# Order of the first loads and of the ahead-of-time keys in a two-layer Perceiver kernel

## Chip, cores and metric

One Trainium2 chip, one core of it (core 0). The metric is the device time of one execution in microseconds (us), the median of several runs. All data are float32 except a few 16-bit integer tiles in the quantized feed-forward layer.

## What is computed

The input is `x`, 64 sequences of 32 rows with 256 features, and a context `ctx` of 64 sequences with 257 rows of 256 features. Six residual steps follow one another, each on a layer-normalized `x`:

```
x = x + L0_xattn(norm(x), ctx)   # causal 32 x 257: only the first 32 context rows count; 16 heads of 16
x = x + L0_attn(norm(x))         # causal attention by offsets, position bias, sigmoid gate
x = x + L0_ffn(norm(x))          # gate/up/down with fake quantization: act_qdq needs max|.| over the whole tensor
x = x + L1_xattn(norm(x), ctx)   # full cross-attention over all 257 context rows
x = x + L1_attn(norm(x))         # causal attention with a Pluecker-line bias
x = x + L1_ffn(norm(x))          # ternary-weight network 256 -> 1024 -> 1024 -> 1024 -> 256
```

In `L0_ffn` each `act_qdq` divides by the largest absolute value of a whole tensor. So the layer has five points (`QX, QG, QU, QS, QO`) at which every column must have been reduced on VectorE and combined over the partitions on GpSimd before anything is scaled; their scales are announced on the semaphore `f0_scale`, 1 to 5.

## The kernel before, in words

The 2048 rows of `x` are 16 tiles (`T`) of 128 rows, kept in SBUF for the whole kernel. The program is written engine by engine: SyncE (the DMA queue), TensorE, ScalarE, VectorE and GpSimd each have one instruction stream in a fixed, hand-written order, and semaphores order them among each other. An instruction waits at the head of its own engine's stream, so whatever stands behind it waits too.

**Attention stages.** `run_lanes` runs the first cross-attention (X0), the first self-attention (A0) and, later, the second self-attention (A1). Four tiles go through a stage together as four lanes, shifted against each other by a quarter of the round, and there are four rounds. Round 0 is unrolled; rounds 1 to 3 are a hardware loop, in which the round number `i` is a register. A tile of X0 begins on VectorE with the statistics (`d_norm`, L1312 and L1315), goes over GpSimd (`rsqrt`, L1804 to L1810) to ScalarE (`a_scale`, L1004), and then to TensorE, which turns it (`p_turn`, L545) and projects it with the X0 weights (`p_project`, L533). The X0 keys and values come from the first 32 context rows of each sequence (`ctxk`).

**First loads (L398 to L423).** SyncE issues all the loads of the start in one row: two tiles of `x`; seven constants, counted on `in_const`; the four X0 weights; `ctxk` of the four lanes; the other 14 tiles of `x`, counted on the same semaphore `in_x`; six later constants; and then all the weights up to A1 and `c_last`. VectorE waits for all seven constants (L1451), makes four small tiles from them (L1452 to L1455), and waits for `in_x` at 32, that is for both loads of `x`, before the first statistics (L1456). TensorE, ScalarE and GpSimd wait for all seven constants as well.

**Keys ahead (L424 to L457, L834 to L852, L1150 to L1181).** Of each group of four sequences, the second cross-attention needs the keys of the fourth one made ahead: there are 16 such projections `j`, in the time of the `L0_ffn` stage. SyncE loads the context `j` (256 KB, `load_ahead`, L432) into one of three buffers; TensorE projects it (L847, eight matmuls) into PSUM bank `(j+1) % 8`; ScalarE evacuates it (`stage_ahead`, L1155, two instructions) into one of four buffers; SyncE stores it to DRAM (`store_ahead`, L437). The queue's order is

```
for j in range(T):
    if j + 3 < T: wait k_ready >= j+1; load_ahead(j+3)
    if j == 10:   wait f0_gj >= 2; load c_ctx[0..3]
    if j >= 1:    store_ahead(j-1)      # waits for k_copied >= j
```

From `j = 8` on, projection `j` also waits for the evacuation of `j-8+1` (its bank), and `stage_ahead(j)` for the store of `j-4` (its buffer). `c_ctx[0..3]` are the contexts of the first four sequences of the second cross-attention. They lie where `gates[0]` and `gates[1]` lay, so their loads wait for the conversions that read these (`f0_gj` at 2).

**Conversions.** ScalarE turns `ups[f]` and `gates[f]`, f = 0 to 5, into 16-bit integers (`f0_up_int` L1141, `f0_gate_int2` L1146, 128x2048 each); VectorE multiplies each pair and reduces its maximum (L1561, then L1492). Two pairs of conversions are held back until `f0_scale` is 3 and 4. `stage_ahead` stands between them in ScalarE's stream: 0 to 3 ahead of the conversions; 4 and 5, then 6, 7 and 8, one group ahead of each of f = 2 to 5; 9 to 15 behind.

**What follows.** GpSimd subtracts the last row from `c_ctx` 0 to 2 (`c_shift`, L1886), and only then comes to `all_max(QO)` (L1852), the reduction over partitions behind the fifth scale. Its instruction is one of another kind than GpSimd's ordinary tensor operations; between the two kinds the trace shows a `MODIFY_POOL_CONFIG` entry. ScalarE, after key 15, evacuates the values of the last rows (L1188) and the keys and values of sequence 0 (L1195, L1201), then waits for `f0_scale` 5 and begins `f0_out_round(0)` (L1182, six instructions). Behind each of these VectorE finishes the quantization (L1488), and TensorE begins the down projection (`f0_down`, L709). Before that TensorE has, in this order: projection 15, the last rows' values, `c_keys(0)` (L731), `c_values(0)` (L737), `c_keys(1)`, `c_values(1)`.

Of the kernel before, what the change touches and what calls it, by code (L numbers as in the profile page):

```python
# [12 lines left out]
ACT = mybir.ActivationFunctionType  # L13
AX = mybir.AxisListType

P = 128
# [4 lines left out]
S = 257  # L21
# [6 lines left out]
NL = 4  # L28
# [15 lines left out]
def perceiver(nc, A, out):  # L44
    ctx = ExitStack()
    with ctx:
        def sb(name, shape, dt=F32):
            return ctx.enter_context(nc.sbuf_tensor(name, shape, dt))

        def sem(name):  # L50
            return ctx.enter_context(nc.semaphore(name))
# [208 lines left out]

        magic = sb("magic", [P, 1])

        ps = ctx.enter_context(nc.psum_tensor("ps", [P, 8, 512], F32))


        in_const, in_later_const = sem("in_const"), sem("in_later_const")
        in_x = sem("in_x")
        in_w = {k: sem(f"in_w_{k}") for k in ("x0", "a0", "nat", "x1", "a1", "ffn")}
# [43 lines left out]

        c_last_in, c_vl_ps, c_vl_done, c_kl_done = map(sem, ("c_last_in", "c_vl_ps", "c_vl_done", "c_kl_done"))
        ctx_in = [sem(f"ctx_in{i}") for i in range(4)]
        ahead_stored = [sem(f"ahead_stored{i}") for i in range(4)]
        k_loaded = sem("k_loaded")
        (k_ready, k_copied, ctx_shifted, v_ready, v_copied, c_s, c_max, c_exp, c_rinv, c_nrm, c_pt, c_ptc,
# [69 lines left out]
        BIAS_V = {X0: colb[:, BV0, :], A0: colb[:, BVA, :], A1: a1_bv[:, :]}  # L387
        N_CONST, N_LATER_CONST = 7, 6
        xl = x[:, :, :].rearrange("p (i l) d -> p i l d", l=NL)
# [7 lines left out]
        def _(sp):  # L397
            sp.dma_start(x[:, 0:2, :], A["x"][:, 0:2, :]).then_inc(in_x, 16)  # L398
            for d, n in ((ident, "ident"), (par, "par"), (mask_hr, "mask_hr"), (mask4, "mask4"),
                         (causal, "causal"), (colb, "colb"), (rowb, "rowb")):  # L400
                sp.dma_start(d[:], A[n]).then_inc(in_const, 16)
# [6 lines left out]

            for l in range(NL):
                load_ctxk(l, 0)  # L410
            sp.dma_start(x[:, 2:T, :], A["x"][:, 2:T, :]).then_inc(in_x, 16)
            for d, n in ((posmask, "posbias"), (a1_bv, "a1_bv"), (a1_bqk, "a1_bqk"), (plscale, "plscale"),
                         (plsign, "plsign"), (w3s, "w3s")):
                sp.dma_start(d[:], A[n]).then_inc(in_later_const, 16)
            for d, n in ((a0_wqkv, "a0_wqkv"), (a0_wg, "a0_wg"), (a0_wout, "a0_wout")):
# [23 lines left out]
            def load_keys(i):  # L439

                after(sp, c_s, 2 * SPT * i)
                sp.dma_start(c_kT[3][:, :, 0:S - 1], k_ahead[i]).then_inc(k_loaded, 16)

# [3 lines left out]
            for j in range(T):  # L447
                if j + 3 < T:
                    sp.wait_ge(k_ready, j + 1)
                    load_ahead(j + 3)  # L450
                if j == 10:
                    sp.wait_ge(f0_gj, 2)
                    for n in range(4):
                        sp.dma_start(c_ctx[n], A["ctxT"][n]).then_inc(ctx_in[n], 16)
                if j >= 1:
                    store_ahead(j - 1)
# [67 lines left out]
        def _(pe):  # L524
# [252 lines left out]
            def c_step(i, u, first, last):  # L777
                n = SPT * i + u
                after(pe, c_exp, G * n)
                if u == 3:  # L780
                    pe.wait_ge(k_loaded, 16 * (i + 1))
                else:
                    pe.wait_ge(k_copied, key_no(3 * i + u))
# [87 lines left out]
            pe.wait_ge(n_q2, 1)  # L871
            pe.wait_ge(c_kl_done, 1)
            pe.wait_ge(c_vl_done, 2)
# [118 lines left out]
        def _(act):  # L992
            af = nc.scalar.activation

            def a_scale(kind, l, n):
# [168 lines left out]
            act.wait_ge(c_vl_done, 1)  # L1164
            stage_ahead(0, 1, 2, 3)
            act.wait_ge(f0_scale, 3)
# [4 lines left out]
            f0_gate_int2(1)  # L1171
            for f, js in zip(range(2, NF0), ((4, 5), (6,), (7,), (8,))):
                stage_ahead(*js)
                f0_up_int(f)
                f0_gate_int2(f)
            stage_ahead(*range(9, T))

# [68 lines left out]
            act.wait_ge(c_x, T)  # L1246
            act.wait_ge(consts_made, 2)
            run_lanes(act, SLOTS1, [
# [53 lines left out]
        def _(dve):  # L1302
# [4 lines left out]
            def d_norm(kind, l, i, n):  # L1307

                if kind == A0:
                    dve.wait_ge(s["x_updated"], tile(i, l))  # L1310
                    stand(dve, "dve")
                v.bn_stats(stats[l][:, :], xl[:, i, l, :]).then_inc(s["stats_ready"], 1)  # L1312
                dve.wait_ge(s["stats_ready"], tile(n, l))
                stand(dve, "dve")
                v.bn_aggr(mv[l][:, :], stats[l][:, :]).then_inc(s["mv_ready"], 1)  # L1315
# [37 lines left out]

            def d_mask(kind, l, i, n):
                dve.wait_ge(s["scores_ready"], tile(n, l))
                mk = posmask if kind == A0 else causal
                if kind != A1:

                    grid = dict(c=4, w=2, k=2 * L)
                    raw = ps[:, 2 * l:2 * l + 2, 0:D].rearrange("p w (c k) -> p w c k", k=2 * L)  # L1360
                    v.tensor_tensor(sc[l].rearrange("p h k -> p (h k)").rearrange("p (c w k) -> p w c k", **grid), raw,
                                    mk[:, :].rearrange("p (c w k) -> p w c k", **grid), ALU.add)\
                        .then_inc(s["scores_masked"], 1)
                    return
                v.scalar_tensor_tensor(sc[l].rearrange("p c k -> p (c k)"), bank[l][0], 0.25, mk[:, :],
                                       ALU.mult, ALU.add).then_inc(s["scores_masked"], 1)
# [87 lines left out]
            for n, at in enumerate((BQ0, BQA)):  # L1454
                v.tensor_scalar(qb[:, n, :], colb[:, at, :], 0.25, None, ALU.mult).then_inc(gate_bias_ready, 1)  # L1455
            dve.wait_ge(in_x, 32)  # L1456

            def enter_a0():
                dve.wait_ge(in_later_const, 16 * N_LATER_CONST)
                v.tensor_tensor(posmask[:, :], posmask[:, :], causal[:, :], ALU.add).then_inc(later_made, 1)  # L1460
# [205 lines left out]
            for u in (0, 1, 3):  # L1666
                r = v.tensor_copy(c_kT[u][:, :, S - 1], colb[:, BK1, :])
            r.then_inc(c_kl_done, 1)
            dve.wait_ge(f0_x, 1 + 1)
# [26 lines left out]
            r.then_inc(consts_made, 1)  # L1696
            dve.wait_ge(consts_made, 2)
            run_lanes(dve, SLOTS1, [
# [98 lines left out]
        def _(pool):  # L1797
# [14 lines left out]
            def bias(l, i, n, k):  # L1812

                pool.wait_ge(s["xn_ready"], tile(n, l))
                p.tensor_tensor(xl[:, i, l, :], xl[:, i, l, :], rowb[:, k, :], ALU.add)\
                    .then_inc(s["x_biased"], 1)
# [113 lines left out]
            last_rsqrt(T - 1)  # L1930
            pool.wait_ge(consts_made, 2)
            pool.wait_ge(later_made, 3)
# [130 lines left out]
```

## Time and profile before

| | us |
|---|---|
| runs: median (lowest to highest of 3) | 1612.7 (1610.29 to 1613.74) |
| the profiled execution, its own time | 1612.98 |
| its span, first to last instruction | 1611.2 |
| TensorE busy | 1465.7 (91%) |
| VectorE busy | 898.6 (56%) |
| ScalarE busy | 712.6 (44%) |
| GpSimd busy | 501.1 (31%) |
| mean granted TensorE clock | 0.978 of full |

How to read it: "busy" is the time in which the engine had an instruction in execution; the share is an average over stages that have different limits. Times within the trace count from the start of the span. In rows of the timeline the first number is the start, the second the length, `x24` means 24 like instructions drawn together, and the bracket tells how long the engine had been idle before and what ended that. The queue's rows (SPq) are the issue of a transfer and not its landing. The kernel's time is a little longer than the span (1.8 us here).

### The profile page before, as it was taken

To read this page: it belongs to the slowest core of one execution; us is meant where nothing else is said; L and a number is where in the kernel's file an instruction comes from. 1 tells how busy PE (TensorE), PEld (TensorE's weight loads), DVE (VectorE), ACT (ScalarE), POOL (GpSimd) and SP (SyncE) were. 2 spreads that over 40 slices of the span, in tenths; PEclk is the share of its full clock that TensorE was granted. 3 is DMA by queue.
4 is the path that set the end of the run, shared out by engine and by line. 5 is a ranking of instruction groups with operands and counts; after the bars stand their busy time and mean duration, and the time that the engine had idled before them with its cause. 6 is when DMAs were issued, how large, how long until landed. Compare 5 with 4: busy or idle time off the path is not lost.

```text
span 1611.2 us, 32991 instructions
## 1 busy us (share of the span) xinstructions
PE 1465.7 (91%) x12564; PEld 1131.0 (70%) x12564; DVE 898.6 (56%) x1897; ACT 712.6 (44%) x1763; POOL 501.1 (31%) x693
## 2 busy tenths in 40 slices
PE   3998996997799999999996788699999999999999
PEld 3887775445677777777773566458867885886887
DVE  2898997479536666666664688634234323422432
ACT  3887775388635554555552455322212212121221
POOL 1444552000125965975652777300000000000000
PEclk9999999998999999999997999899999999999999
DMA  7000000003304153146110000104412330441230
GB/s 285 24 11 2 1 0 21 0 0 118 118 29 143 52 186 127 52 156 221 59 40 1 1 1 0 46 0 142 167 71 92 138 137 13 156 165 59 92 137 13
DMA packets 60509, 123.98 MB, mean 77 GB/s; under 512 B 5008, under 2 KB 15760, under 8 KB 57872
## 3 DMA queue, kind: packets, MB, share of 16 engines
q1 hardware_dynamic: 60432, 122.94, 21.9%
q8 instruction: 50, 0.82, 0.2%
q14 instruction: 27, 0.22, 0.0%
HBM read 108.24 MB, written 14.68 MB: 76 GB/s over the span
## 4 chain that ended last, share of the span: by engine, by line
PE 71%; DVE 11%; POOL 8%; issue 4%; ACT 3%; DMA 1%; SPq 0%; DVEq 0%; POOLq 0%; ACTq 0%
PE ps L921 23%; PE ps L533 17%; PE ps L539 5%; PE ps L737 5%; PE ps L731 4%; PE ps L972 3%; PE ps L757 3%; POOL R L1912 2%; DVE R L1323 2%; DVE R L1618 2%; PE ps L709 2%; POOL R L1894 2%; PE ps L768 2%; PE ps L847 1%; PE ps L602 1%
## 5 line engine op out<-in xcount | busy, mean ns | idle before, releaser
L921 PE MATMUL ps<-R 128*128 128x256 f32 x1792 | 388.6, 379 | 3.4 <-DVE R L1751 3.4
L921 PEld LDWEIGHTS ps<-R 128*128 128x128 f32 x1792 | 340.0, 190 | 52.2 <-issue 6.5
L533 PE MATMUL ps<-R 128*128 128x128 f32 (+1 forms) x1344 | 308.2, 389 | 6.4 <-DVE R L1488 4.8
L533 PEld LDWEIGHTS ps<-R 128*128 128x128 f32 x1344 | 191.3, 195 | 119.3 <-issue 109.6
L1209 ACT ACTIVATE R<-ps,c_nmx 128x257 f32<-128x257 f32 x256 | 118.2, 474 | 126.6 <-DVE c_nmx L1642 126.6
L1894 POOL TENSOR_TENSOR R<-R,c_inv 128x1024 f32<-128x1024 f32 x64 | 121.1, 1892 | 133.2 <-DVE c_inv L1653 133.2
L1618 DVE COPY R<-ps 128x512 f32<-128x512 f32 x128 | 88.1, 688 | 82.1 <-PE ps L757 80.8
L737 PE MATMUL ps<-x_wv,R 128*128 128x256 f32 x512 | 121.1, 379 | 0.0
L1972 POOL TENSOR_SCALAR g_ve<-g_mv 128x4 f32<-128x4 f32 x4 | 0.9, 237 | 345.5 <-DVE g_mv L1713 345.5
L737 PEld LDWEIGHTS ps<-x_wv,R 128*128 128x128 f32 x512 | 92.5, 190 | 10.1
L731 PE MATMUL ps<-R,x_wk 128*128 128x256 f32 x384 | 95.7, 391 | 0.0
L1278 ACT ACTIVATE R<-R,ffn_s 128x256 f32<-128x256 f32 x32 | 16.2, 508 | 167.5 <-DVE R L1758 167.5
L757 PE MATMUL ps<-ident,R 128*128 128x128 f32 x512 | 80.1, 280 | 9.6 <-POOL R L1894 3.8
L1642 DVE TENSOR_REDUCE c_nmx<-ps 128x2 f32<-128x514 f32 x128 | 82.5, 686 | 1.7 <-PE ps L747 1.5
L1265 ACT ACTIVATE R<-ps,ffn_s 128x512 f32<-128x512 f32 x32 | 22.0, 687 | 126.0 <-PE ps L533 126.0
L757 PEld LDWEIGHTS ps<-ident,R 128*128 128x128 f32 x512 | 60.9, 143 | 23.6 <-issue 7.7
L731 PEld LDWEIGHTS ps<-R,x_wk 128*128 128x128 f32 x384 | 68.9, 189 | 12.2 <-issue 0.4
L1492 DVE TENSOR_REDUCE amax<-R 128x1 f32<-128x512 f32 (+1 forms) x60 | 58.4, 1002 | 32.8 <-ACT R L1104 32.3
L1886 POOL TENSOR_TENSOR R<-R 128x512 f32<-128x512 f32 x64 | 68.7, 1074 | 25.2 <-DMA R<-in_ctxT 25.2
L1201 ACT ACTIVATE R<-ps 128x512 f32<-128x512 f32 x64 | 38.4, 600 | 75.3 <-PE ps L737 75.3
L1736 DVE SCALAR_TENSOR_TENSOR R<-ps,ffn_s,R 128x512 f32<-128x512 f32 x32 | 24.0, 750 | 73.0 <-ACT R L1265 73.0
L768 PEld LDWEIGHTS ps<-R 128*32 128x32 f32 x2048 | 32.4, 110 | 44.6 <-DVE R L1618 32.5
(211 smaller groups left out, 2526.2 us busy)
## 6 DMA issues: line engine op xcount, KB each, us to landing
R<-quadrant_sums SPq DMA_DIRECT2D x32, 1024.0 KB, 6.8
R<-in_f_hq SPq DMA_DIRECT2D x32, 768.0 KB, 4.6
R<-in_ctxT SPq DMA_DIRECT2D x64, 257.0 KB, 2.7
R<-in_f_hq SPq DMA_DIRECT2D x8, 1024.0 KB, 8.8
quadrant_sums<-R SPq DMA_DIRECT2D x8, 1024.0 KB, 8.3
R<-in_ctxT SPq DMA_DIRECT2D x16, 256.0 KB, 3.4
k_ahead<-R SPq DMA_DIRECT2D x16, 256.0 KB, 3.4
R<-k_ahead SPq DMA_DIRECT2D x16, 256.0 KB, 3.1
```

The costliest lines, as they stand in the source:

```text
L533: r = mm(dst, w[:, ki, fo * P:(fo + 1) * P], src[:, ki, :], start=(ki == 0), stop=(ki == KI - 1))
L539: r = mm(dst, src[:, ki, :], w[:, ki], start=(ki == 0), stop=(ki == KI - 1))
L731: r = mm(ps[:, 4, fo * D:(fo + 1) * D], x1_wk[:, ki, fo * P:(fo + 1) * P], c_ctx[u][:, ki, 0:2 * P], start=(ki == 0), stop=(ki == KI - 1))
L737: r = mm(ps[:, 5, c * D:(c + 1) * D], c_ctx[u][:, ki, c * P:(c + 1) * P], x1_wv[:, ki, :], start=(ki == 0), stop=(ki == KI - 1))
L757: r = tr(ps[:, 6, at:at + P], c_p[par][:, g, c * P:(c + 1) * P], ident[:])
L768: r = mm(ob[g * L:(g + 1) * L, ki * 2 * L:(ki + 1) * 2 * L], c_v[u][:, c, cols], c_pT[:, g, c, ki * 2 * L:(ki + 1) * 2 * L], start=(c == 0 ...
L921: r = mm(ps[:, 4 * (g % 2) + bk, half * HALF:(half + 1) * HALF], f_wr[g % 3][:, w, ki * P:(ki + 1) * P], src[:, k, ki, :], start=(ki == 0) ...
L1209: af(c_p[par][:, g, :], ps[:, g, 0:S], ACT.Exp, bias=c_nmx[par][:, g:g + 1], accum_out=c_sum[par][:, g:g + 1]).then_inc(c_exp, 1)
L1618: v.tensor_copy(c_pT[:, 2 * k:2 * k + 2, :, :].rearrange("p g c t -> p (g c t)"), ps[:, 6, :])\
L1642: v.tensor_reduce(c_nmx[u % 2][:, 2 * half:2 * half + 2], ps[:, 2 * half:2 * half + 2, 0:S], AX.X, ALU.max, negate=True).then_inc(c_max, 1)
L1886: p.tensor_tensor(c_ctx[u][:, :, 0:S - 1], c_ctx[u][:, :, 0:S - 1], c_ctx[u][:, :, S - 1:S].broadcast_to([P, KI, S - 1]), ALU.subtract).th ...
L1894: p.tensor_tensor(c_p[u % 2][:, :, 0:S - 1], c_p[u % 2][:, :, 0:S - 1], c_inv[u % 2][:, :].unsqueeze(2).broadcast_to([P, G, S - 1]), ALU.m ...
```

## The change

It changes no arithmetic. The first loads are put in another order and counted on other semaphores; a first activation is added at the top of ScalarE's stream; the waits for `causal` and `rowb` move to where they are read; in the loop of the keys ahead, the loads of `c_ctx[0..3]` move from `j == 10` to `j == 6`; and of the evacuations six instead of four stand ahead of the conversions, with the others in other places between them. Two semaphores are merged into others (`k_loaded` into `c_last_in`, `c_kl_done` into `consts_made`), with their counts raised to fit. The diff, cut to its core:

```diff
 SyncE
-            sp.dma_start(x[:, 0:2, :], A["x"][:, 0:2, :]).then_inc(in_x, 16)
-            for d, n in ((ident, "ident"), (par, "par"), (mask_hr, "mask_hr"), (mask4, "mask4"),
-                         (causal, "causal"), (colb, "colb"), (rowb, "rowb")):
+            sp.dma_start(x[:, 0:NL, :], A["x"][:, 0:NL, :]).then_inc(in_x, 16)
+            for d, n in ((ident, "ident"), (colb, "colb"), (mask4, "mask4"), (mask_hr, "mask_hr"), (par, "par")):
                 sp.dma_start(d[:], A[n]).then_inc(in_const, 16)
...
-            for l in range(NL):
-                load_ctxk(l, 0)
-            sp.dma_start(x[:, 2:T, :], A["x"][:, 2:T, :]).then_inc(in_x, 16)
+            load_ctxk(0, 0)
+            load_ctxk(1, 0)
+            for d, n in ((causal, "causal"), (rowb, "rowb")):
+                sp.dma_start(d[:], A[n]).then_inc(in_add, 16)
+            load_ctxk(2, 0)
+            load_ctxk(3, 0)
+            sp.dma_start(x[:, NL:T, :], A["x"][:, NL:T, :]).then_inc(in_later, 16)
             for d, n in ((posmask, "posbias"), (a1_bv, "a1_bv"), (a1_bqk, "a1_bqk"), (plscale, "plscale"),
                          (plsign, "plsign"), (w3s, "w3s")):
-                sp.dma_start(d[:], A[n]).then_inc(in_later_const, 16)
+                sp.dma_start(d[:], A[n]).then_inc(in_later, 16)
...
-                if j == 10:
+                if j == 6:
                     sp.wait_ge(f0_gj, 2)
                     for n in range(4):
                         sp.dma_start(c_ctx[n], A["ctxT"][n]).then_inc(ctx_in[n], 16)
 ScalarE
+            act.wait_ge(consts_made, 1)
+            af(act_start[:, :], minus_half[:, 0:1], ACT.Identity)
...
-            stage_ahead(0, 1, 2, 3)
+            stage_ahead(0, 1, 2, 3, 4, 5)
             act.wait_ge(f0_scale, 3)
             for f in range(2):
                 f0_up_int(f)
             act.wait_ge(f0_scale, 4)
             f0_gate_int2(0)
             f0_gate_int2(1)
-            for f, js in zip(range(2, NF0), ((4, 5), (6,), (7,), (8,))):
+            for f, js in zip(range(2, NF0), ((6, 7), (8, 9), (10,), (11,))):
                 stage_ahead(*js)
                 f0_up_int(f)
                 f0_gate_int2(f)
-            stage_ahead(*range(9, T))
+            stage_ahead(*range(12, T))
 VectorE
+                elif not isinstance(i, int):
+                    dve.wait_ge(in_later, 16 * N_LATER)
+                    stand(dve, "dve")
                 v.bn_stats(stats[l][:, :], xl[:, i, l, :]).then_inc(s["stats_ready"], 1)
...
             def d_mask(kind, l, i, n):
+                if kind == X0:
+                    dve.wait_ge(in_add, 32)
...
-            dve.wait_ge(in_x, 32)
+            dve.wait_ge(in_x, 16)
 GpSimd
             def bias(l, i, n, k):
+                if k == BO0:
+                    pool.wait_ge(in_add, 32)
```

## Rows read from the trace of the kernel before

**Rows 1.** Timeline, 0 to 40 us: start, length, engine, line, operation [idle before <- releaser]
```profile
0.74 0.40 SPq L398 DMA_DIRECT2D x<-in_x  x1
...
4.50 0.43 SPq L403 DMA_DIRECT2D R<-in_x_wq  x1
...
7.95 0.17 DVE L1452 TENSOR_SCALAR hbg<-colb 128x2 f32<-128x2 f32 x1 [6.85 <-DMA rowb<-in_rowb]
...
17.79 0.43 DVE L1312 BATCH_NORM_STATS2 stats<-x 128x6 f32<-128x256 f32 x1 [9.47 <-DMA x<-in_x]
...
20.79 1.28 ACT L1004 ACT_TABLE_LOAD   x1 [20.79 <-POOL nmr L1810]
...
22.82 0.66 PE L545 MATMUL ps<-ident,R 128*128 128x128 f32 x2 [22.82 <-ACT R L1004]
...
23.95 5.49 PE L533 MATMUL ps<-R 128*128 128x128 f32 x24 [0.47 <-ACT R L1018]
...
31.88 2.94 PE L533 MATMUL ps<-R 128*128 128x128 f32 x24 [0.47 <-ACT R L1018]
```

**Rows 2.** Timeline of TensorE, 385 to 470 us
```profile
392.17 8.32 PE L847 MATMUL ps<-R,x_wk 128*128 128x256 f32 x24 [8.30 <-DMA R<-in_ctxT]
...
411.50 5.38 PE L847 MATMUL ps<-R,x_wk 128*128 128x256 f32 x16 [3.40 <-DMA R<-in_ctxT]
...
426.75 20.96 PE L709 MATMUL ps<-R 128*128 128x256 f32 x96 [2.07 <-DVE R L1488]
```

**Rows 3.** Timeline of the DMA queue, 385 to 470 us
```profile
388.16 0.33 SPq L437 DMA_DIRECT2D k_ahead<-R  x1
...
403.37 2.03 SPq L454 DMA_DIRECT2D R<-in_ctxT  x4
```

**Rows 4.** Timeline of ScalarE, 335 to 470 us
```profile
379.73 3.90 ACT L1141 ACTIVATE R<-R,qinv 128x2048 int16<-128x2048 f32 x2 [5.13 <-DVE qinv L1483]
...
387.32 1.54 ACT L1155 ACTIVATE R<-ps,kb_ahead 128x256 f32<-128x256 f32 x4
...
404.14 2.03 ACT L1146 ACTIVATE R<-R,qinv 128x2048 int16<-128x2048 f32 x1
...
421.75 4.33 ACT L1182 ACTIVATE R<-R,magic,qinv 128x512 f32<-128x512 f32 x6
```

**Rows 5.** DMA issues: what is loaded, count, KB each, median us to landing
```profile
rowb<-in_rowb SPq DMA_DIRECT2D x1, 512.0 KB, 3.9
...
R<-in_x_wq SPq DMA_DIRECT2D x1, 256.0 KB, 4.3
...
R<-in_x_wo SPq DMA_DIRECT2D x1, 256.0 KB, 5.6
...
par<-in_par SPq DMA_DIRECT2D x1, 2.0 KB, 2.1
```

**Rows 6.** Stage table, 70 to 93 us: busy us (count) by engine, clock, DMA share, GB/s
```profile
70.00:93.00 23.00, 22.84 (x333) 19.19 (x332) 20.85 (x42) 20.35 (x56) 10.02 (x20) 1.00 0.07 19
```

**Rows 7.** Timeline of VectorE, 385 to 470 us
```profile
408.22 3.07 DVE L1561 TENSOR_TENSOR R<-R 128x2048 f32<-128x2048 int16 x1
...
413.64 0.16 DVE L1565 TENSOR_REDUCE pmax<-amax 128x1 f32<-128x6 f32 x1
...
419.21 0.16 DVE L1571 TENSOR_TENSOR qinv<-qinv,qus 128x1 f32<-128x1 f32 x1
```

**Rows 8.** Line L454 by itself (the four loads of `c_ctx`)
```profile
DMA to landing us min/median/max: 3.3/4.1/4.4
```

**Rows 9.** Timeline of GpSimd, 255 to 300 and 385 to 470 us
```profile
278.34 0.38 POOL L1852 PARTITION_ALL_REDUCE allmax<-pmax  x1 [7.25 <-DVE pmax L1508]
...
418.21 0.38 POOL L1852 PARTITION_ALL_REDUCE allmax<-pmax  x1 [6.03 <-issue]
```

**Rows 10.** Line L1852 by itself: x count: ns min/median/max, first and last start us
```profile
L1852 POOLq MODIFY_POOL_CONFIG  x4: 6/8/11, 271.0 to 412.4; - x4
```

**Rows 11.** Stage table, 903 to 1036 us (second self-attention)
```profile
903.00:1036.00 133.00, 111.17 (x1515) 85.95 (x1514) 110.90 (x193) 75.96 (x190) 93.79 (x182) 1.00 0.00 1
```

More of the change, by code:

```diff
@@ L261, in perceiver @@
         magic = sb("magic", [P, 1])
+        act_start = sb("act_start", [P, 1])
         ps = ctx.enter_context(nc.psum_tensor("ps", [P, 8, 512], F32))
-        in_const, in_later_const = sem("in_const"), sem("in_later_const")
-        in_x = sem("in_x")
+        in_const, in_later = sem("in_const"), sem("in_later")
+        in_x, in_add = sem("in_x"), sem("in_add")
         in_w = {k: sem(f"in_w_{k}") for k in ("x0", "a0", "nat", "x1", "a1", "ffn")}
@@ L311, in perceiver @@
         f0_or, f0_oq, f0_y, f0_x = map(sem, ("f0_or", "f0_oq", "f0_y", "f0_x"))
-        c_last_in, c_vl_ps, c_vl_done, c_kl_done = map(sem, ("c_last_in", "c_vl_ps", "c_vl_done", "c_kl_done"))
+        c_last_in, c_vl_ps, c_vl_done = map(sem, ("c_last_in", "c_vl_ps", "c_vl_done"))
         ctx_in = [sem(f"ctx_in{i}") for i in range(4)]
         ahead_stored = [sem(f"ahead_stored{i}") for i in range(4)]
-        k_loaded = sem("k_loaded")
         (k_ready, k_copied, ctx_shifted, v_ready, v_copied, c_s, c_max, c_exp, c_rinv, c_nrm, c_pt, c_ptc,
@@ L387, in perceiver @@
         BIAS_V = {X0: colb[:, BV0, :], A0: colb[:, BVA, :], A1: a1_bv[:, :]}
-        N_CONST, N_LATER_CONST = 7, 6
+        N_CONST, N_LATER = 5, 7
         xl = x[:, :, :].rearrange("p (i l) d -> p i l d", l=NL)
@@ L441, in load_keys @@
                 after(sp, c_s, 2 * SPT * i)
-                sp.dma_start(c_kT[3][:, :, 0:S - 1], k_ahead[i]).then_inc(k_loaded, 16)
+                sp.dma_start(c_kT[3][:, :, 0:S - 1], k_ahead[i]).then_inc(c_last_in, 16)
             sp.wait_ge(wT_turned, 9)
@@ L780, in c_step @@
                 if u == 3:
-                    pe.wait_ge(k_loaded, 16 * (i + 1))
+                    pe.wait_ge(c_last_in, 16 * (i + 2))
                 else:
@@ L871, in _ @@
             pe.wait_ge(n_q2, 1)
-            pe.wait_ge(c_kl_done, 1)
+            pe.wait_ge(consts_made, 2)
             pe.wait_ge(c_vl_done, 2)
@@ L1246, in _ @@
             act.wait_ge(c_x, T)
-            act.wait_ge(consts_made, 2)
+            act.wait_ge(consts_made, 3)
             run_lanes(act, SLOTS1, [
@@ L1455, in _ @@
                 v.tensor_scalar(qb[:, n, :], colb[:, at, :], 0.25, None, ALU.mult).then_inc(gate_bias_ready, 1)
-            dve.wait_ge(in_x, 32)
+            dve.wait_ge(in_x, 16)
             def enter_a0():
-                dve.wait_ge(in_later_const, 16 * N_LATER_CONST)
+                dve.wait_ge(in_later, 16 * N_LATER)
                 v.tensor_tensor(posmask[:, :], posmask[:, :], causal[:, :], ALU.add).then_inc(later_made, 1)
@@ L1667, in _ @@
                 r = v.tensor_copy(c_kT[u][:, :, S - 1], colb[:, BK1, :])
-            r.then_inc(c_kl_done, 1)
+            r.then_inc(consts_made, 1)
             dve.wait_ge(f0_x, 1 + 1)
@@ L1696, in _ @@
             r.then_inc(consts_made, 1)
-            dve.wait_ge(consts_made, 2)
+            dve.wait_ge(consts_made, 3)
             run_lanes(dve, SLOTS1, [
@@ L1930, in _ @@
             last_rsqrt(T - 1)
-            pool.wait_ge(consts_made, 2)
+            pool.wait_ge(consts_made, 3)
             pool.wait_ge(later_made, 3)
```

## The prediction

> **What bounds the kernel now.** I read the timeline of the first 40 us, then the stage tables, then the timelines of the five engines around 380 to 430 us. TensorE is busy for 91% of the span, so the change can only gain where TensorE waits. The diff touches two such places, and the reader should find what ends the wait in each.
>
> *The start.* TensorE does nothing until 22.82 us [rows 1]. VectorE's first real work, the statistics at 17.79, was released by a load of `x`, after an idle time of 9.47. The two loads of `x` share one count, so the first tile waits for the last. Before that, VectorE had waited until 7.95 for `rowb`, a constant read much later. From 17.79 to TensorE's start it is 5.03 us, and 1.28 of them are a table load on ScalarE, which starts only once its first real work is released [rows 1].
>
> *The middle.* TensorE stands still for 8.30, 3.40 and 2.07 us [rows 2]. The first two waits are for contexts of the keys ahead. The queue is blocked: it stores key 4 only at 388.16 [rows 3], behind ScalarE's four conversions, because keys 4 and 5 are evacuated at 387.32 [rows 4]. Then the four `c_ctx` loads enter at 403.37 [rows 3] ahead of the last keys' contexts. The third wait ends when `f0_out_round(0)`, begun at 421.75 [rows 4], has passed VectorE.
>
> **Part 1, the first loads.** The queue issues one load each 0.47 us (0.74 to 4.50 is eight issues) [rows 1]. Four tiles of `x` (512 KB) go first; `rowb`, of that size, took 3.9 [rows 5], so they land at about 4.6. The fifth constant is issued at 0.74 + 5 x 0.47 = 3.1 and lands 2.1 later [rows 5], at 5.2. VectorE then makes its four small tiles (about 0.4, an estimate between its 7.95 row and nothing that waits) and starts the statistics at 5.6. Add 5.03, less the 1.28 of the table load, which now runs in ScalarE's idle start: 9.4. TensorE also needs the four X0 weights. They are issued at 3.6 to 5.0. In the run of before, the first landed at 4.50 + 4.3 = 8.8 and the last (issued three later, at 5.9) 5.6 after its issue, at 11.5 [rows 5]: 0.9 a weight. With `causal` and `rowb` out of their way, four times 0.9 behind the 4.6 of `x` gives 8.2; with the old 5.6 the last lands at 5.0 + 5.6 = 10.6. I take 9.5, since the queue ahead is about half as long (0.6 MB, not 1.1), and keep 9.4 to 10.6. **Gain 22.8 - 9.5 = 13.3**, with ends 12.2 and 13.4.
>
> The first 24 matmuls took 5.49 where the next 24 took 2.94 [rows 1]: TensorE starts slow out of idleness. I carry that over unchanged; it can be 1 us either way.
>
> What is late next: `ctxk` of lane 0 is issued 0.5 behind the last weight and lands about 1 us behind it, while TensorE first does the turn and the query half of the projection (over 2 us). `rowb` lands at about 12.5, so GpSimd's first bias waits some 3 us instead of nothing; behind it on GpSimd is the root for lane 2, which is due only some 11 us after the start. `causal` lands at about 11 and is first read at 18. The later constants and the rest of `x` keep their place in the queue (land by 20) and are first asked for in round 1, at about 31. The new wait with its mark stands 12 times ahead of the statistics in rounds 1 to 3. Nothing in the trace prices it alone. TensorE is busy 22.84 of 23.00 in this stage and VectorE 20.85 [rows 6], so it mostly hides; ends 0 and 12 x 0.16 = 1.9 (0.16 is the length of VectorE's smallest instructions [rows 7]); I take a **loss of 0.3**, nearer to the row that shows TensorE full.
>
> **Part 2, the keys ahead.** Evacuations 4 and 5 move into the 5.13 us for which ScalarE waits ahead of its first conversion at 379.73 [rows 4]. TensorE had finished projection 8 at 392.17 - 8.30 = 383.9 [rows 2]; at 1.75 for eight matmuls (96 in 20.96 [rows 2]) projection 5 was done by about 378.5. Two instructions at 0.385 (four in 1.54 [rows 4]) end at 379.3. They cost nothing, with 0.4 to spare. The queue is now free to store 4 and load 9, and then waits for two conversions of each kind: 379.73 + 4 x 1.95 = 387.5. The four `c_ctx` loads follow at 0.5 each (2.03 for four [rows 3]), and then store 5, load 10, store 6, load 11, store 7, load 12, at 0.6 each. With 4.1 to 4.4 to landing [rows 8], context 10 is there at about 394.5 and 12 at 397. TensorE is idle from 385.7 to 394.5, as long as in the 8.30 us gap, behind which 24 matmuls took 8.32 instead of 5.2 [rows 2]. With such a slow start of 3 us, projections 10 to 15 end at 408 or 409.
>
> ScalarE has one evacuation (0.77) more ahead of f = 3, 4 and 5, and key 9's buffer waits for store 5 (lands about 393.8, 0.4 late). Before, it delivered f = 5 at 404.14 + 2.03 = 406.2 and VectorE took it at 408.22 [rows 4, 7], 2.0 later. So ScalarE may slide by 1.2 and VectorE, which is the bound here, still ends at 413.8 [rows 7]. Its 3.07 us product at 408.22 ran beside `c_shift`; the next-to-like ones would now stretch earlier, which I count as equal (0.8 either way). ScalarE evacuates keys 12 to 15 from 407.0 to 410.1; last rows, `c_keys(0)`, `c_values(0)` follow on TensorE (0.9 + 1.75 + 1.75) and are evacuated by 413.5 to 415.
>
> Then the fifth scale. GpSimd's reduction began at 418.21 [rows 9], 4.4 behind the maximum that VectorE had ready at 413.8, and the profile names no releaser. The last `MODIFY_POOL_CONFIG` entry is at 412.4 [rows 10], when `c_shift` was done: 5.8 us. An earlier one is at 271.0, and that reduction began at 278.34, straight behind VectorE's maximum [rows 9, 10]: where the entry comes early, the 6 us are hidden. With `c_ctx` loaded 16 us earlier, `c_shift` is done at about 396 and the 6 us pass before 413.8. So the reduction starts at 413.9, and the scale, which came 419.37 - 418.21 = 1.16 behind its start [rows 7, 9], at 415.0.
>
> The Trainium skill (GPSIMD Engine Reference, 2.1 Instruction dispatch) says that the first call to a freshly loaded kernel additionally pays about 6 us. Read by the letter, that speaks against this gain, since the call would pay it wherever it stands; the total would be the one of rival A. The two reductions in the rows do not bear that reading out.
>
> `f0_out_round(0)` starts at 415.0 instead of 421.75, and `f0_down` 5.0 behind it (426.75 - 421.75 [rows 2, 4]), at 420.0. **Gain 6.7**; ends 2.4 (rival A) and 7.5. All that follows hangs on `f0_down` as before and moves with it.
>
> **Sum.** 13.3 - 0.3 + 6.7 = 19.7. From the profiled execution's own 1612.98 that is 1593.3; the median of the runs is 0.3 lower, so I give 1593.0. The least that a measurement of this kernel can tell from no change is about 0.2%, 3.2 us.
>
> **Rivals.**
> A. *The 6 us on GpSimd are paid at the call.* For: the 6.03 idle at 418.21 has no other releaser. Against: 278.34. Then the scale comes at 419.4 as before, and only ScalarE's 2.4 us are won: 13.3 - 0.3 + 2.4 = 15.4, **1597.3**. Chance 0.07.
> B. *The start is held by its loads.* The weights come at 10.6 or later, since the queue is full and every engine fetches its program through the same DMA engines while the other loads still come in; some steps of round 0 wait. Gain of part 1 10.5 instead of 13.3: **1595.8**. Against: TensorE also ran under the same flood from 23 to 34 us without new idle. Chance 0.12.
> C. *TensorE starts `f0_down` slow.* Its idle time before it grows from 2.07 to about 3.6; behind 2.07 it ran at full rate, behind 3.40 it started slow [rows 2]. Price 1.5 to 3 us: **1595.3**. Chance 0.1.
> D. *Slower: the granted clock falls in the second self-attention.* There TensorE has small gaps all along and still ran at full clock from 903 to 1036, busy 111.17 of 133 [rows 11]. If the 20 us shift put these gaps so that half rate was granted there, each us of the stage would hold 1.67 us of work, a loss of 0.67. It decides from 30 us of the stage on (20 / 0.67); over 60 us it costs 40 and gives **1633**. Against: nothing in the change touches that stage. Chance 0.02.
>
> **How the numbers follow.** The forecast has 0.69. Its own range is 1591 to 1595 (12.2 to 13.4, 0 to 1.9, 0.8 for the products, 1 for the slow start). A, B and C lie at 1595 to 1597.5. So 1590.5 to 1597.5 leaves out D and small tails. Faster by over 0.2%: all but D and unnamed mishaps, 0.96; within 0.2% 0.02; slower 0.02.
>
> **What would show it.** Right: the first statistics at 5 to 6 us without an idle time ended by `x`, the table load within the first 2 us, TensorE from 9.5 on; round 1 without a wait on DMA; keys 4 and 5 evacuated before 379.7 less 13; a `MODIFY_POOL_CONFIG` some 16 us ahead of the last reduction, which follows VectorE's maximum directly; the last contexts no longer what TensorE waits for; 5 us from L1182 to L709. Wrong: a reduction that still starts 4 us late (A), an idle time of TensorE ended by weights or `ctxk` in the first 40 us (B), `f0_down`'s first matmuls at twice their length (C), a granted clock under 1.00 behind 890 us for longer than before (D), or a VectorE chain that ends later than 413.8 less 13.

## The result, and the profile after

The changed kernel took **1593.87 us** (median of 4 runs, 1591.85 to 1595.79), beside 1612.97 for the kernel before: a ratio of 0.9884, 95% interval 0.9867 to 0.9902. The forecast was 1593.0, range 1590.5 to 1597.5. The traced execution's span is 1594.0 us, 17.2 less than the 1611.2 of before. The runs of one kernel differ by up to 5 us, so I compare traces stretch by stretch, and times by medians. All traces are compared with the one trace of the kernel before.

**The start.** From the timeline of the changed kernel, 0 to 40 us (the rows that answer to [rows 1]):

```profile
0.73 1.28 ACT L998 ACT_TABLE_LOAD   x1 [0.73 <-PEq L2068]
...
3.56 0.43 SPq L402 DMA_DIRECT2D R<-in_x_wq  x1
...
5.53 0.17 DVE L1462 TENSOR_SCALAR hbg<-colb 128x2 f32<-128x2 f32 x1 [4.43 <-DMA par<-in_par]
...
5.82 0.42 DVE L1320 BATCH_NORM_STATS2 stats<-x 128x6 f32<-128x256 f32 x1
...
9.57 0.66 PE L548 MATMUL ps<-ident,R 128*128 128x128 f32 x2 [9.57 <-ACT R L1009]
...
10.70 5.34 PE L536 MATMUL ps<-R 128*128 128x128 f32 x24 [0.47 <-ACT R L1023]
...
12.36 0.73 POOL L1827 TENSOR_TENSOR x<-x,rowb 128x256 f32<-128x256 f32 x1 [2.11 <-DMA rowb<-in_rowb]
```

The statistics no longer wait for `x`, the table load is over at 2.0, and TensorE starts at 9.57. GpSimd's first bias waits for `rowb`, and nobody waits for GpSimd. From the list of DMA issues, which tell KB each and us to landing:

```profile
x<-in_x SPq DMA_DIRECT2D x1, 512.0 KB, 3.9
...
R<-in_x_wo SPq DMA_DIRECT2D x1, 256.0 KB, 4.2
```

**The middle.** The changed kernel's timelines by engine, 355 to 425 us, for TensorE, ScalarE, the queue, VectorE and GpSimd (they answer to [rows 2 to 4, 7, 9]):

```profile
384.90 8.87 PE L850 MATMUL ps<-R,x_wk 128*128 128x256 f32 x32 [9.02 <-DMA R<-in_ctxT]
394.19 3.69 PE L850 MATMUL ps<-R,x_wk 128*128 128x256 f32 x16 [0.42 <-DMA R<-in_ctxT]
399.27 1.10 PE L536 MATMUL ps<-c_last,x_wv 128*128 128x64 f32 x8 [1.39 <-ACT R L1160]
```
```profile
367.96 0.84 ACT L1160 ACTIVATE R<-ps,kb_ahead 128x256 f32<-128x256 f32 x2 [1.64 <-PE ps L850]
369.39 3.90 ACT L1146 ACTIVATE R<-R,qinv 128x2048 int16<-128x2048 f32 x2 [0.59 <-DVE qinv L1493]
...
384.13 0.84 ACT L1160 ACTIVATE R<-ps,kb_ahead 128x256 f32<-128x256 f32 x2 [1.10 <-DMA k_ahead<-R]
...
404.53 4.34 ACT L1187 ACTIVATE R<-R,magic,qinv 128x512 f32<-128x512 f32 x6
```
```profile
368.49 0.59 SPq L440 DMA_DIRECT2D k_ahead<-R  x1
...
377.10 2.06 SPq L457 DMA_DIRECT2D R<-in_ctxT  x4
```
```profile
403.04 0.16 DVE L1575 TENSOR_REDUCE pmax<-amax 128x1 f32<-128x6 f32 x1
...
404.33 0.16 DVE L1581 TENSOR_TENSOR qinv<-qinv,qus 128x1 f32<-128x1 f32 x1
```
```profile
403.34 0.38 POOL L1864 PARTITION_ALL_REDUCE allmax<-pmax  x1 [18.36 <-DVE pmax L1575]
```

Keys 4 and 5 are evacuated 0.59 us before the first conversion may start. Store 4 leaves at 368.49, and the `c_ctx` loads follow at 377.10. The reduction starts 0.14 us behind the end of VectorE's maximum; before, it was 4.4. The 8.3 us idle time of TensorE is not gone, it is 9.02 now, but nothing that sets the end waits behind it: TensorE later waits 1.39 for an evacuation, and not for a context. In the chain of waits two ends meet: the fifth scale is written at 404.49, and ScalarE comes free of the keys and values at 404.53. So both chains were shortened to the same point, and shortening one further would gain nothing by itself.

**Where the lead comes from and goes.** This table takes the same matmul, by its place in TensorE's order, in two traces, and tells how many us earlier it starts than in the trace of the kernel before (whose time for it heads the column):

```
matmul of before at     22.8   35.0   49.6  125.9  131.0  269.3  284.7  365.8  434.6  the last
changed kernel          13.3   13.4   13.0   12.7   11.2    9.3   10.4   10.3   17.2   17.2
 the same, second trace 13.2   14.0   13.0   12.8   12.8   11.1   12.2   12.2   19.1   18.9
 the same, third trace  13.2   13.9   12.9   12.7   12.7   10.9   12.1   12.0   18.9   18.9
loads_only              12.7   13.8   12.8   12.6   12.6   12.5   13.4   12.8   12.5   12.4
keys_only                0.0    0.4    0.4    0.4    0.4   -3.1   -1.9   -2.2    4.6    4.4
evac_only                0.4    0.4    0.4    0.4    0.4    0.4    1.3    0.8    7.4    7.2
ctx_only                 0.4    0.6    0.6    0.6    0.6    0.7    0.7    0.8    1.3    0.9
late_shift              13.3   13.9   12.9   12.6   11.1   11.2   11.7   11.6   12.0   11.7
no_first_act            11.9   11.9   10.9   10.7    9.1    7.3    8.5    8.4   15.2   15.3
consts_back             10.0   10.1   10.1   10.1   10.1   10.1   10.1   10.2   16.9   17.0
one_wait                13.4   13.4   13.3   13.1   13.1   12.3   13.4   13.3   20.2   19.8
one_wait_again          13.2   14.1   14.0   13.8   12.2   11.3   12.4   12.3   19.2   18.8
wo_later                13.2   14.1   14.0   13.8   12.2   11.2   12.4   12.3   19.2   18.7
```

In the first trace the 13.3 of part 1 is there at the start and has shrunk to 10.3 by 365.8 us; part 2 then adds 6.9 (10.3 to 17.2).

### The profile page after: what moved, and what is told of

Its sections match the earlier page's. It is cut to its first block, busy times and chain, and to the rows that moved or that the text cites. A ratio compares the mean times of both kernels' runs of the same rounds, so it can differ in the third digit from the quotient of the medians.

```text
span 1594.0 us, 33033 instructions
## 1 busy us (share of the span) xinstructions
PE 1467.2 (92%) x12564; PEld 1131.5 (71%) x12564; DVE 899.1 (56%) x1897; ACT 713.7 (45%) x1764; POOL 501.8 (31%) x693
## 4 chain that ended last, share of the span: by engine, by line
PE 72%; DVE 11%; POOL 8%; issue 4%; ACT 3%; DMA 1%; DVEq 0%; SPq 0%; POOLq 0%; ACTq 0%
PE ps L924 23%; PE ps L536 17%; PE ps L542 5%; PE ps L740 5%; PE ps L734 4%; PE ps L975 3%; PE ps L760 3%; PE ps L712 3%; POOL R L1924 2%; DVE R L1331 2%; DVE R L1628 2%; POOL R L1906 2%; PE ps L771 2%; PE ps L605 1%; POOL R L1898 1%
## 5 line engine op out<-in xcount | busy, mean ns | idle before, releaser
L740 PEld LDWEIGHTS ps<-x_wv,R 128*128 128x128 f32 x512 | 92.5, 190 | 10.1
L734 PEld LDWEIGHTS ps<-R,x_wk 128*128 128x128 f32 x384 | 68.9, 189 | 12.2 <-issue 0.4
```

The costliest lines, as they stand in the source:

```text
L734: r = mm(ps[:, 4, fo * D:(fo + 1) * D], x1_wk[:, ki, fo * P:(fo + 1) * P], c_ctx[u][:, ki, 0:2 * P], start=(ki == 0), stop=(ki == KI - 1))
L740: r = mm(ps[:, 5, c * D:(c + 1) * D], c_ctx[u][:, ki, c * P:(c + 1) * P], x1_wv[:, ki, :], start=(ki == 0), stop=(ki == KI - 1))
```

## The experiments

All were timed in five rounds beside the kernel before, in three groups, each on one chip; the median of before was 1611.62, 1613.07 and 1611.52 in them. The changed kernel itself was in the first and third.

**1. The changed kernel again.** No edit.

> The changed kernel once more, unchanged, for the spread between executions and a second trace. Theory (2 us of the start's gain are lost to spells of half granted clock whose place differs from one execution to the next): the matmul at 127.7 us of before is 12.5 us earlier than in the kernel before, with or without the drop to 11.3 behind it that the first trace shows, and the time lies within 1591.8 to 1595.8. Rival (the loss belongs to the changed order of work): the same drop of 1.2 us in the same place.

> The changed kernel again, for comparison with one_wait_again, wo_later and consts_back on the same chip: 1594, with a spread of 2 us either way.

Measured: 1594.28 (ratio 0.9890, 0.9875 to 0.9906) and 1593.73 (0.9886, 0.9871 to 0.9901). The first trace's lead drops by 1.5 us between the matmuls at 125.9 and 131.0 (12.7 to 11.2); neither of the new traces has this drop. Both medians are inside the range that was expected. The stage table shows why, the same 3.4 us of the first trace and of the third (span, then busy us by engine; the column of 0.51 and 1.00 is the granted clock):

```profile
114.80:118.20 3.40, 3.40 (x72) 2.84 (x57) 2.70 (x5) 1.83 (x5) 0.00 (x0) 0.51 0.02 5
```
```profile
114.80:118.20 3.40, 3.40 (x85) 3.11 (x70) 2.87 (x7) 2.13 (x6) 0.00 (x0) 1.00 0.02 5
```

Follows: at the change of stage the clock is granted at half (1.2 instead of 2.4 GHz) in some executions of the same kernel and not in others, with TensorE busy throughout. In the 3.4 us before, TensorE had been busy for 1.70 us in the one and 1.71 in the other. The spell costs 1.5 us. It isn't shown that the change has no part in it: of the ten traces with the new order of the first loads five have this spell, of the four traces with the old order none has.

**2. Each part alone.** `loads_only` is the changed kernel with `j == 10` and the old places of the evacuations; `keys_only` is the kernel before with

```diff
-                if j == 10:
+                if j == 6:
-            stage_ahead(0, 1, 2, 3)
+            stage_ahead(0, 1, 2, 3, 4, 5)
-((4, 5), (6,), (7,), (8,))   and   range(9, T)
+((6, 7), (8, 9), (10,), (11,))   and   range(12, T)
```

> The changed kernel with its part 2 undone (c_ctx at j == 10, four evacuations ahead of the conversions). Theory (the two parts add up): TensorE starts at 9.6 us, 13.3 us earlier than in the kernel before; some 2 to 3 us of that are lost again by 365 us, as in the changed kernel's trace, so the whole is 10 to 11.5 us faster than before, 1601.5 to 1603. Rival (what is won at the start is kept whole, and the shortfall comes from part 2): 13 us faster, 1600 or less.

> The kernel before with part 2 alone (c_ctx at j == 6, six evacuations ahead, the others moved). Theory: 6.7 to 6.9 us faster than before, 1606.2; the last reduction on GpSimd starts within 0.2 us of VectorE's maximum. Rival (part 2 gains only ScalarE's 2.4 us, or needs part 1's shift): 2.4 us faster or less, 1610.5.

Measured: `loads_only` 1601.28 (0.9942, 0.9928 to 0.9955), 10.3 less than before; `keys_only` 1604.93 (0.9954, 0.9940 to 0.9967), 6.7 less. Together 17.0; the changed kernel in the same group was 17.3 less. The parts add up within the spread of the runs, and the medians agree with the expectations. But part 1 was forecast at 13.0 in the prediction, and 10.3 is 2.7 less (interval 7.3 to 11.6). The loss of 2 to 3 us by 365 us, on which the expectation for `loads_only` rested, is not in its trace: the lead is still 12.8 there and 12.4 at the end, so for this run the number agreed and the mechanism didn't. Trace and medians differ because the traced execution of the kernel before (1612.98) lies 1.4 us above its median in this group, and that of `loads_only` (1600.6) 0.7 below its own. In `keys_only` the reduction stood ready, as the timeline of GpSimd shows:

```profile
415.90 0.38 POOL L1852 PARTITION_ALL_REDUCE allmax<-pmax  x1 [18.36 <-DVE pmax L1565]
```

**3. The head start of GpSimd's switch taken away.**

```diff
-            for u in range(3):
+            for u in range(2):
                 c_shift(u, 0)
+            pool.wait_ge(f0_o, NF0)
+            c_shift(2, 0)
             all_max(QO)
```

> The changed kernel, with GpSimd's third c_shift held back until VectorE's last product (semaphore f0_o at 6), some 2.3 us ahead of the maximum. It takes away only the head start of the entry MODIFY_POOL_CONFIG. Theory (the gap of about 6 us starts at the entry and was what bounded the fifth scale): c_shift ends at about 401.8, the entry follows, the reduction starts at about 407.6 instead of 403.34, and the kernel is 4.2 us slower than the changed one, about 1598. Rival (the gap is paid at the call, or comes from something else than the entry): the reduction starts at 403.4 as before or the time moves by less than 1 us.

Measured: 1599.59 (0.9923, 0.9909 to 0.9936), 5.3 slower than the changed kernel beside it. By the table its lead grows by 0.3 us from 365.8 to 434.6, where that of the changed kernel grows by 6.9: 6.5 us in the traces. Of `late_shift`, the timelines of GpSimd and TensorE, and the reduction's line by itself (count: shortest, median, longest in ns, first and last start):

```profile
398.96 1.04 POOL L1898 TENSOR_TENSOR R<-R 128x512 f32<-128x512 f32 x1 [16.25 <-DVE R L1571]
406.16 0.38 POOL L1864 PARTITION_ALL_REDUCE allmax<-pmax  x1 [6.16 <-issue]
```
```profile
412.36 23.39 PE L712 MATMUL ps<-R 128*128 128x256 f32 x96 [6.54 <-DVE R L1498]
```
```profile
L1864 POOLq MODIFY_POOL_CONFIG  x4: 11/11/11, 259.8 to 400.2; - x4
```

The entry at 400.2 comes directly behind the held `c_shift`, and the reduction 6.0 us behind the entry, though VectorE's maximum was ready at 401.4. In the changed kernel the entry was at 385.2 and 18 us stood between them unused:

```profile
L1864 POOLq MODIFY_POOL_CONFIG  x4: 8/10/11, 260.1 to 385.2; - x4
```

Follows: the 6 us run from the entry and not from the call. The Trainium skill's sentence that the first call pays about 6 us (GPSIMD Engine Reference, 2.1 Instruction dispatch) gives the right length, 5.8 and 6.0 here, but a call that comes late enough pays none of it. Rival A is refuted. Both 5.3 and 6.5 are more than the 4.2 expected: the late scale costs 4.1 of the 6.5, and the other 2.4 come from `f0_down`'s 96 matmuls, which took 23.39 us instead of 20.96 behind an idle time of 6.54. That is rival C's mechanism, seen behind a longer idle time than the 3.6 it was forecast for. The stage table of `late_shift` has the clock at half there:

```profile
410.60:417.40 6.80, 5.04 (x12) 4.08 (x13) 3.85 (x9) 6.52 (x11) 0.00 (x0) 0.51 0.00 0
417.40:424.00 6.60, 6.60 (x32) 5.80 (x32) 1.50 (x4) 0.00 (x0) 0.00 (x0) 1.00 0.00 0
```

**4. Part 2 halved.** `evac_only`: the kernel before with the moved evacuations and `j == 10`. `ctx_only`: with `j == 6` and the old evacuations.

> The kernel before with the evacuations moved (six ahead of the conversions, the others between), but c_ctx still loaded at j == 10. Theory (each half of part 2 removes one of two chains that end nearly together): the keys end early, but c_ctx comes later than in the full part 2, so c_shift ends some 6 us ahead of VectorE's maximum or later and the scale at 415 to 417; 4 to 6.5 us faster than before. Rival (only both together give anything): under 1 us.

> The kernel before with c_ctx loaded at j == 6 and the evacuations as they were. Theory: GpSimd's reduction starts straight behind the maximum and the scale comes at 415.0, but the keys still end late (their queue was blocked until 388.2, and now c_ctx goes ahead of all the loads from 10 on), so f0_out_round(0) starts when c_values(0) is evacuated, at 419 to 421.5; 0 to 2.5 us faster. Rival (the fifth scale alone was the bound): 6 us faster.

Measured: `evac_only` 1607.43 (0.9965, 0.9953 to 0.9977), 5.6 less than before; `ctx_only` 1611.26 (0.9991, 0.9982 to 1.0000), 1.8 less. In `evac_only` the gain lies in the range, but the scale came at 413.5 and not at 415 to 417, and ScalarE, free at 414.4, was the last. In `ctx_only` the scale was early and ScalarE late: the timelines of GpSimd and ScalarE are

```profile
412.34 0.38 POOL L1852 PARTITION_ALL_REDUCE allmax<-pmax  x1 [14.32 <-DVE pmax L1565]
```
```profile
413.47 0.84 ACT L1155 ACTIVATE R<-ps,kb_ahead 128x256 f32<-128x256 f32 x2 [4.48 <-PE ps L847]
...
420.47 2.92 ACT L1182 ACTIVATE R<-R,magic,qinv 128x512 f32<-128x512 f32 x4
```

In `evac_only` the unblocked queue alone brings the `c_ctx` loads forward, to 393.52 from 403.37 [rows 3], so that the switch is hidden as well:

```profile
393.52 2.03 SPq L454 DMA_DIRECT2D R<-in_ctxT  x4
```
```profile
412.32 0.38 POOL L1852 PARTITION_ALL_REDUCE allmax<-pmax  x1 [9.79 <-DVE pmax L1565]
```

Follows: the moved evacuations carry nearly all of part 2, since the early ones free the queue, which frees both chains (the two early ones weren't tried without the other moves). From 365.8 to 434.6 the lead grows by 6.9 us in `keys_only`, 6.5 in `evac_only` and 0.5 in `ctx_only` (table). So moving the `c_ctx` loads to `j == 6` adds about 0.3 us to the evacuations by the traces; the medians, 6.7 and 5.6 of two groups, can't tell that from nothing.

**5. The first activation.** The changed kernel without `act.wait_ge(consts_made, 1)` and the activation behind it.

> The changed kernel without the activation at the top of ScalarE's stream. Theory: the table load stands again ahead of the first scaling, TensorE starts at 10.85 instead of 9.57, and the kernel is 1.3 us slower, 1595. Rival (the weights land at about 9 to 10 us and hide it in part): under 0.5 us slower.

Measured: 1596.53 (0.9892, 0.9877 to 0.9907), 16.5 less than before, where the changed kernel was 17.3 and 17.8 less in the other groups. In the trace it costs the whole table load, on the start itself:

```profile
8.88 1.28 ACT L1007 ACT_TABLE_LOAD   x1 [8.88 <-POOL nmr L1818]
10.17 0.60 ACT L1007 ACTIVATE R<-x,nmr,rstd 128x256 f32<-128x256 f32 x1
10.92 0.66 PE L548 MATMUL ps<-ident,R 128*128 128x128 f32 x2 [10.92 <-ACT R L1007]
```

Theory right by the trace (10.92 instead of 9.57); the medians of different groups don't resolve 1.3 us.

**6. The constants' order.** The changed kernel with `causal` and `rowb` back among the constants, counted on `in_const`.

> The changed kernel with causal and rowb loaded ahead of the X0 weights again and counted on in_const, as before; x stays split into 4 and 12 tiles. Theory (both halves of part 1 count: x's split gives the larger one, the order of the constants the smaller): VectorE starts its small tiles at about 8.8 us and the weights land at about 12.4, so TensorE starts at 12.5 to 13 instead of 9.6; 3 us slower than the changed kernel, about 1597. Rival (the split of x is all that counted): under 0.5 us slower.

Measured: 1595.97 (0.9906, 0.9893 to 0.9920), 2.2 slower than the changed kernel beside it. Its timeline:

```profile
8.77 0.17 DVE L1459 TENSOR_SCALAR hbg<-colb 128x2 f32<-128x2 f32 x1 [7.67 <-DMA rowb<-in_rowb]
...
12.80 0.66 PE L547 MATMUL ps<-ident,R 128*128 128x128 f32 x2 [12.80 <-ACT R L1008]
```

TensorE starts 3.2 later. So of the 13.3 won at the start, 3.2 are the constants' order, 1.3 the table load and the rest, 8.8, is put down to the split of `x` (a difference, no run of its own). But this kernel keeps its 10.1 without any loss up to 285 us (see the table), though it has the same 12 waits on VectorE. By themselves they don't shrink the lead.

**7. The waits on VectorE.** The changed kernel with one wait in round 0 in place of the 12 with their marks:

```diff
-                elif not isinstance(i, int):
-                    dve.wait_ge(in_later, 16 * N_LATER)
-                    stand(dve, "dve")
...
             def d_norm_out(kind, l, i, n):
+                if kind == X0 and l == 0 and isinstance(i, int) and i == 0:
+                    dve.wait_ge(in_later, 16 * N_LATER)
```

> The changed kernel with VectorE waiting for the later loads once, in round 0 of the first stage (at lane 0's normalization of the output), instead of 12 times with a mark in rounds 1 to 3. Theory (these 12 waits cost 0.07 us each, the 0.9 us by which the lead in the trace shrinks from 13.4 to 12.5 between 30 and 128 us): the lead over the kernel before stays at 13.3 to 13.4 until 127 us, and the kernel is 0.9 us faster than the changed one. Rival (the waits are hidden and the lead shrinks for another reason, the loads beside it): the same lead of 12.5 at 127 us.

> one_wait once more, beside the changed kernel on the same chip. Theory (a wait and a mark less, 12 times): 0.6 to 1 us faster than the changed kernel, 1593.3. Rival (the first difference of 0.6 us was the spread between runs): no difference.

> The changed kernel with one wait for the later loads (as in one_wait) and with the output weight of the first stage loaded behind rowb on a count of its own, waited for at the first output projection. Theory (in some executions, as in the trace where TensorE's first idle time ended with that weight at 9.62, the start hangs on the weights): TensorE starts at 9.4 in every execution; 0 to 0.5 us faster than one_wait. Rival (it delays something else): slower than one_wait.

Measured: `one_wait` 1593.48 (0.9878, 0.9863 to 0.9893) and 1594.10 (0.9888, 0.9873 to 0.9903); `wo_later` 1593.10 (0.9881, 0.9866 to 0.9896); the changed kernel beside the last two 1593.73. No difference that these runs can tell. In `wo_later` TensorE started at 9.58 and not at 9.4. In the traces the lead between 35.0 and 49.6 falls by 0.4, 1.0 and 1.0 us in the changed kernel and by 0.1 at most with one wait. So the theory of 0.07 us a wait is wrong: the loss is made in a single place, at the entry of round 1. First the changed kernel's first trace, then its third, then `one_wait_again`, timelines of all engines:

```profile
34.50 1.82 POOL L1827 TENSOR_TENSOR x<-x,rowb 128x256 f32 x1
34.50 1.23 DVE L1337 TENSOR_TENSOR R<-R,mask_hr 128x1024 f32<-128x1024 f32 x1 [0.28 <-issue]
```
```profile
33.96 0.73 POOL L1827 TENSOR_TENSOR x<-x,rowb 128x256 f32 x1
33.97 1.80 DVE L1337 TENSOR_TENSOR R<-R,mask_hr 128x1024 f32<-128x1024 f32 x1 [0.28 <-issue]
```
```profile
33.48 1.17 DVE L1334 TENSOR_TENSOR R<-R,mask_hr 128x1024 f32<-128x1024 f32 x1
...
33.65 1.04 POOL L1819 TENSOR_TENSOR nmr<-nmr,rstd 128x1 f32<-128x1 f32 x1
34.65 0.73 POOL L1826 TENSOR_TENSOR x<-x,rowb 128x256 f32 x1
```

VectorE's product takes 1.80 where GpSimd's bias starts 0.01 us ahead of it, and 1.17 where VectorE is first; then it is GpSimd's small operation that stretches, 1.04 instead of 0.19, and nobody waits for that. With 0.28 of a late start this makes the 0.9 to 1.0 us, once. In the first trace the two start at the same 34.50, the bias stretches to 1.82 and VectorE's product takes 1.23, so that only about 0.4 us are lost. The 0.28 us of idle time ahead of the product stand in all six traces that have both the 12 waits and the new waits for `causal` and `rowb`, and in none of the four with the new loads that lack one of the two (`one_wait` twice, `wo_later`, `consts_back`). So neither set of waits costs this by itself, but both together delay VectorE once and let GpSimd be first; what VectorE does in the 0.28 us isn't shown. In `one_wait_again` and `wo_later` what is won is lost again to the half-clock spell at the change of stage (13.8 to 12.2). The trace of `one_wait` has no such spell and ends 19.8 us ahead, the largest lead of all; by the medians no version here is shown to beat the changed kernel.

## Why the prediction was right, point by point

- **Start at 9.5:** 9.57 and, in the other two traces, 9.6. The three steps: four tiles of `x` landed after 3.9, as taken from `rowb`; the constants were there at 5.5 (5.2 forecast), the statistics at 5.8 (5.6), TensorE 3.75 behind them, as forecast. The weights landed at 4.99 + 4.2 = 9.2, inside the 8.2 to 10.6 given. They were nearly the bound: in the second trace of the changed kernel and in `loads_only` it was the last weight that ended TensorE's idle time, at 9.62 and 10.13. Rival B was this close, but cost 0.6 us at most.
- **The slow start of TensorE, 1 us either way:** the first 24 matmuls took 5.34 us in the first trace and 4.52 in the third.
- **Loss of 0.3 for the new waits:** too small, and the mechanism was wrong. It wasn't 12 small costs. The two sets of new waits together delay VectorE once, at 34 us, by 0.28 us, and there it meets GpSimd: 0.4 us lost in the first trace, 1.0 in the others. I had not counted such a collision. With the half-clock spells and small steps the lead fell from 35.0 to 365.8 us by 3.1, 1.8 and 1.9 us in the three traces. The ends of 0 to 1.9 hold the last two and not the first.
- **Part 2, 6.7:** 6.7 alone by medians, and 6.9 in the traces. The evacuations of 4 and 5 fit ahead of the conversions (0.59 spare, 0.4 forecast). ScalarE slid by more than forecast, since store 5 kept key 9 waiting for 1.10 us and not 0.4. It still delivered in time, and the whole string of VectorE's conversions took 27.9 us (375.27 to 403.20) beside 28.2 before. The fifth scale came 1.15 behind the reduction's start, and `f0_down` 5.0 behind L1187: 409.54 - 404.53.
- **Idle time ahead of `f0_down`, 3.6 forecast:** it was 2.19, at full clock. The key chain ended at the late end of my bound, so `c_values(1)` did too. Rival C did not occur here, and did in `late_shift`.
- **The sum:** 19.7 forecast; by medians 19.1 in the first comparison, and 17.3 and 17.8 in the two later ones; between traces 17.2, 18.9 and 18.9. All lie below the forecast, and the first comparison is the most favourable. The changed kernel's own median, 1593.7 to 1594.3 in all three, stays within 1.3 us of the forecast of 1593.0. What is missing is in part 1 and not in part 2: the losses of the lead above were 1.8 to 3.1 us and not 0.3. In two of the three traces that was partly made good by luck, since TensorE's first 24 matmuls took 4.4 and 4.5 us, and not the 5.49 that I had carried over.
- Rival D: the half-clock spells in the second self-attention kept their place relative to the work (the first begins at 862.3 us before and at 845.2 in the first trace, 23.9 long in both), and the lead at the end is within 0.3 us of the lead before that stage. It was not tried by itself.

## What to carry to other kernels

A count that covers early and late loads together makes the first user wait for the last load, so split it where the use splits, and put an engine's one-time delays (ScalarE's table load, the 6 us behind GpSimd's `MODIFY_POOL_CONFIG`) where that engine has nothing to do. Where a queue serves loads and stores in one order, look for the entry that waits for a slow engine: freeing that one (evacuations ahead of the conversions) moved everything behind it, and was worth more than moving the loads themselves. When two chains end together, shortening only one gives little (`ctx_only`, 1.8 us), and their sum shows only when both are shortened.

## What the runs showed of the hardware

- Ahead of a reduction over partitions, GpSimd's `MODIFY_POOL_CONFIG` starts an interval of about 6 us (5.8 in the kernel before, 6.0 in `late_shift`), in which the reduction doesn't start. The interval runs on while GpSimd waits for a semaphore, so it costs nothing if the entry comes 6 us early. In these traces the entry stands directly behind the last instruction of the other kind. The switch back took 7.1 us (entry at 438.9, next tensor operation at 446.0 in the kernel before); what that costs the kernel wasn't tried. Behind the very first entry, at 19.1 us, the next instruction came 0.1 us later, so not every entry has such an interval.
- Two operations of VectorE and GpSimd that meet: 1.80 instead of 1.17 us on VectorE, or 1.04 instead of 0.19 on GpSimd, by who is first; started together, 1.23 on VectorE and 1.82 instead of 0.73 on GpSimd. A shift of 0.5 us decides it, and with it up to 1 us of the kernel.
- The same program had its clock at half for 3.4 us at the change of stage in some executions and not in others, with TensorE busy in both and alike in the 3.4 us before. It moves a trace by 1.5 us, nearly a quarter of what part 2 is worth, so single traces should be compared stretch by stretch.
